# A quantized feed-forward with the gated product on GpSimd and the up projection's copy on ScalarE

## The reference, cut to what matters

```
def fp4_quant_dequant(x):
    xb = x.reshape(shape[:-1] + (shape[-1] // 16, 16))
    scale = jnp.maximum(jnp.max(jnp.abs(xb), axis=-1, keepdims=True) / 6.0, 1e-12)
    idx = jnp.searchsorted(_MID, jnp.abs(xb / scale))
    return (_GRID[idx] * jnp.sign(xb / scale) * scale).reshape(shape)
def fp4_linear(x, w):
    return jnp.einsum('bsk,nk->bsn', fp4_quant_dequant(x), fp4_quant_dequant(w))
gate = fp4_linear(x, w_gate)          # 128 -> 352
y = fp4_linear(x, w_up)               # 128 -> 352
h = jax.nn.silu(gate) * y
return fp4_linear(h, w_down)          # 352 -> 128
x = x + _L1_ffn_ref(_layernorm(x), ...)
```

## Time and profile before

| | us |
|---|---|
| median of 3 runs | 1462.62 (1462.22 to 1463.78) |
| the profiled execution | 1462.41, of which the span 1460.3 |
| TensorE busy in the span | 1284.1 (88%) |
| VectorE | 1015.8 (70%) |
| ScalarE | 931.7 (64%) |
| GpSimd | 510.8 (35%) |
| granted TensorE clock, mean | 0.943 of full speed |

### The profile page before, as it was taken

One profiled execution on the slowest core, in us unless ns is written; L12 is line 12 of the kernel. 1 busy time (PEld: TensorE's weight loads), 2 busy tenths in 40 slices (PEclk: granted clock), 3 DMA queues, 4 the chain that ended last, 5 costly groups with the idle time before them and its releaser, 6 DMA issues.

```text
span 1460.3 us, 17118 instructions
## 1 busy us (share of the span) xinstructions
PE 1284.1 (88%) x6134; PEld 693.6 (47%) x6134; DVE 1015.8 (70%) x1814; ACT 931.7 (64%) x1200; POOL 510.8 (35%) x358
## 2 busy tenths in 40 slices
PE   6999998999899999666878877899989999986666
PEld 3444453445344544331222222477756767763344
DVE  7788858885888578165776778356548676668895
ACT  4999978997899789432565666545545454433321
POOL 1445534553455344417433441023310000006333
PEclk9999999999999999866898999999999999998877
DMA  8100000000000000100000000000010000000000
GB/s 179 48 1 1 0 0 1 0 1 1 0 1 0 0 1 11 63 1 0 1 1 1 1 1 1 1 1 1 1 55 1 1 0 1 1 1 0 1 8 22
DMA packets 27711, 15.01 MB, mean 10 GB/s; under 512 B 16638, under 2 KB 26476, under 8 KB 27500
## 3 DMA queue, kind: packets, MB, share of 16 engines
q1 hardware_dynamic: 27628, 13.92, 3.6%
HBM read 12.86 MB, written 1.05 MB: 10 GB/s over the span
## 4 chain that ended last, share of the span: by engine, by line
PE 36%; issue 24%; POOL 21%; DVE 16%; ACT 2%; POOLq 0%; DMA 0%; SPq 0%; ACTq 0%; DVEq 0%
POOL ARENA L2145 10%; DVE ARENA L874 7%; POOL ARENA L2150 6%; PE PS L749 4%; PE PS L1066 4%; PE PS L732 4%; PE PS L608 3%; POOL ARENA L2157 3%; PE PS L650 3%; PE PS L1074 2%; PE PS L1097 2%; PE PS L617 2%; PE PS L1089 2%; PE PS L1078 2%; PE PS L1751 1%
## 5 line engine op out<-in xcount | busy, mean ns | idle before, releaser
L1751 PE MATMUL PS<-ARENA 128*128 128x512 f32 x512 | 227.3, 597 | 7.5 <-issue 6.7
L874 DVE TENSOR_REDUCE ARENA<-PS 128x1 f32<-128x512 f32 x256 | 160.1, 682 | 69.3 <-PE PS L617 69.1
L2042 DVE TENSOR_SCALAR ARENA<-PS,ARENA 128x512 f32<-128x512 f32 x256 | 188.1, 748 | 27.5 <-PE PS L1751 9.9
L2145 POOL TENSOR_TENSOR ARENA<-ARENA 128x1024 f32<-128x1024 f32 x64 | 151.5, 2367 | 131.6 <-ACT ARENA L1895 126.7
L794 ACT ACTIVATE ARENA<-PS 128x1024 f32<-128x1024 f32 x128 | 129.2, 1026 | 64.3 <-PE PS L636 64.0
L1751 PEld LDWEIGHTS PS<-ARENA 128*128 128x128 f32 x512 | 95.3, 191 | 117.3 <-issue 113.4
L1879 ACT ACTIVATE ARENA<-ARENA 128x2048 f32<-128x2048 f32 x64 | 119.7, 1905 | 47.6 <-DVE ARENA L2042 47.3
L1887 ACT ACTIVATE ARENA<-ARENA,consts_sb 128x2048 f32<-128x2048 f32 x64 | 127.8, 1996 | 0.4
L1760 PE MATMUL PS<-ARENA 128*64 128x512 f32 x512 | 119.9, 611 | 8.1 <-ACT ARENA L1895 8.1
L1895 ACT ACTIVATE ARENA<-ARENA 128x2048 f32<-128x2048 f32 x64 | 118.3, 1897 | 0.0
L617 PE MATMUL PS<-ARENA 32*128 32x512 bf16 x256 | 81.0, 402 | 39.7 <-DVE ARENA L874 27.9
(11 more groups left out here) (257 smaller groups left out, 2611.7 us busy)
## 6 DMA issues: line engine op xcount, KB each, us to landing
ARENA<-in_window_bias_dram SPq DMA_DIRECT2D x1, 1536.0 KB, 6.5
WKVG<-in_L_attn_W_in_dram SPq DMA_DIRECT2D x3, 448.0 KB, 6.7
X<-in_x_dram SPq DMA_DIRECT2D x4, 256.0 KB, 4.4
W<-in_L_ffn_w_dram SPq DMA_DIRECT2D x1, 1024.0 KB
out_dram<-X SPq DMA_DIRECT2D x4, 256.0 KB, 2.2
WQ<-in_L_attn_W_in_dram SPq DMA_DIRECT2D x2, 448.0 KB, 8.3
BV<-in_L_attn_b_in_dram SPq DMA_DIRECT2D x1, 512.0 KB, 6.8
Wout<-in_L_attn_W_out_dram SPq DMA_DIRECT2D x1, 512.0 KB, 4.8
```

Source lines behind the costliest of these rows:

```text
L874: dve.tensor_reduce(NMX[:, w % 2, t, h:h + 1], bank(("cS", n, j)), AX.X, ALU.max, negate=True).then_inc(sem("c_max"), 1)
L1751: done(pe.matmul(o, SK[:, hd, kt * P:(kt + 1) * P], MQ[:, hd, :], start=True, stop=True), ("S", u, c))
L2042: dve.tensor_scalar(D[:, u % 2, hd, kt, :], bank(("S", u, c)), K2[:, u % 2, kt, hd:hd + 1], 1e-30, ALU.add, ALU.max).then_inc(sem("guarded ...
L2145: pool.tensor_tensor(WPAIR, D[:, u % 2, hd, 0:2], D[:, u % 2, hd, 2:4], ALU.add).then_inc(sem("w_paired"), 1)
```

## The change

ScalarE, after the Silu of a step, also copies the up projection out of PSUM, into a new buffer `UF`. It is laid over `W2`, weights of a stage that is over by then. GpSimd forms the product `HF` = `SG` x `UF`, in the new function `product`: those of steps 0 and 1 first, and then in step n that of step n+1 ahead of the subtraction and the multiplication of step n. `HF` gets a second buffer. VectorE no longer forms the product; it waits for `f_h`, which now comes from GpSimd. The banks of `fU` are free after ScalarE's copy (`f_u`) instead of after the product.

```diff
 def gate_and_up_jobs(n):
-    return [(("fG", n), 2, [("f_silu", n + 1)]), (("fU", n), 2, [("f_h", n + 1)])]
+    return [(("fG", n), 2, [("f_silu", n + 1)]), (("fU", n), 2, [("f_u", n + 1)])]
...
-        HF, at = carve(at, [2, FI])
+        HF, at = carve(at, [2, 2, FI])
+        UF = W2[:].rearrange("p e c d -> p (e c d)")[:, 0:4 * FI].rearrange("p (n t f) -> p n t f", n=2, t=2)
...
+            def product(n):
+                pool.wait_ge(sem("f_silu"), n + 1)
+                pool.wait_ge(sem("f_u"), n + 1)
+                if n >= 2:
+                    pool.wait_ge(sem("f_added"), n - 1)
+                pool.tensor_tensor(HF[:, n % 2], SG[:, n % 2], UF[:, n % 2], ALU.mult).then_inc(sem("f_h"), 1)
+
+            product(0)
             for n in range(STEPSF):
 
+                if n + 1 < STEPSF:
+                    product(n + 1)
                 scratch = X_SCRATCH[n % 2]
                 pool.wait_ge(sem("f_added"), n + 1)
...
             act.activation(SG[:, n % 2], bank(("fG", n))[:, :, 0:FI], ACT.Silu).then_inc(sem("f_silu"), 1)
+            full(act, ("fU", n))
+            act.copy(UF[:, n % 2], bank(("fU", n))[:, :, 0:FI]).then_inc(sem("f_u"), 1)
...
         def hidden(dve, link, n, add):
 
-            dve.wait_ge(sem("f_silu"), n + 1)
-            full(dve, ("fU", n))
-            if n:
-                dve.wait_ge(sem("f_added"), n)
-            dve.tensor_tensor(HF, SG[:, n % 2], bank(("fU", n))[:, :, 0:FI], ALU.mult).then_inc(sem("f_h"), 1)
             if n >= 2:
                 add(n - 2)
             dve.wait_ge(sem("f_h"), n + 1)
-            quantize(dve, link, X_SCRATCH[n % 2], P, HF.rearrange("p t n -> p (t n)"), 2 * FI, None, "f_added",
+            quantize(dve, link, X_SCRATCH[n % 2], P, HF[:, n % 2].rearrange("p t n -> p (t n)"), 2 * FI, None, "f_added",
                      max(n - 1, 0))
```

More of the change, by code:

```diff
@@ L560, in decoder_kernel @@
                      "f_rounded", "f_added", "e_exp", "e_rc", "e_p", "e_pt", "e_o", "xb4", "mask_bias",
-                     "f_weights_in", "f_wq", "f_w", "f_yq", "f_x", "f_silu", "f_h", "f_hq", "f_ht", "x_final"):
+                     "f_weights_in", "f_wq", "f_w", "f_yq", "f_x", "f_silu", "f_u", "f_h", "f_hq", "f_ht", "x_final"):
             sem(name)
```

## The result

The changed kernel takes 1481.51 us (median of 4 runs, 1478.99 to 1484.23) against 1463.20 for the kernel before on the same chip: ratio 1.0121, interval 1.0095 to 1.0146, slower by 14 to 21 us. The forecast was 1480.

A forecast was written before the change was run, and what follows sets the result against it. The last stage was taken to go at VectorE's pace; the change closes a serial chain. Start to 1396.6, six turns 64.3, extras 0.8 and 1.5, end 6.15 give 1469.35, 17.6 later: added to the 1462.62 median, 1480; range 1469 to 1488 us.

The forecast's parts named there:

- The closed loop: Last feed-forward stage: one serial chain through four engines, from one step's GpSimd multiplication to the next's, 10.7 us; 63 in 100.
- turn: From the end of one step's GpSimd multiplication to the next's: forecast 10.7 us, against 8.5 before.
- fX: TensorE's transposes ahead of step 5's gate and up matmuls, forecast to add 0.8 us once.
- the input's quantization: VectorE's quantization of the last batch's input, meeting GpSimd's work in one turn: forecast to add 1.5 us once.
- P: The gated product of a step, now on GpSimd: forecast 1.67 us, with 1.39 as the lower end.
- M: GpSimd's multiplication of a step: 1.39 us in the chain; its last end was forecast 17.6 us later.
- the end: From step 6's to step 7's GpSimd multiplication, with no product ahead: VectorE's remaining quantization, subtraction and multiplication, 6.15 us.
- the start: Step 0's GpSimd multiplication, held by step 1's product, forecast to end at 1396.6 instead of 1392.22 us.
- GU: TensorE's eight gate and up matmuls of a step: 3.78 us, ending 4.83 after the earlier GpSimd multiplication.
- S: GpSimd's subtraction of a step, 1.67 us, forecast to wait behind the next step's product, no longer for VectorE's addition.
- The port rival: The port shared by VectorE and GpSimd alone sets the pace in this stage: 7.8 us a step, 1466 us; 5 in 100.
- The hidden product: Rival: GpSimd's product is hidden by running a step ahead, gaining about 5 to 6 us, 1457; 4 in 100.

The follow-up runs named there:

- P behind M: The changed kernel with GpSimd's product for the next step queued behind the current step's multiplication instead of ahead of its subtraction: 1475.65 us, ratio 1.0066.
- P twice: The changed kernel with a second GpSimd product of the same size, into unused columns, ahead of the real one in every step: 1499.56 us, ratio 1.0224.
- copy twice: The changed kernel with ScalarE's copy of the up projection made twice in every step, first into unused columns: 1491.10 us, ratio 1.0165.
- two ahead: The changed kernel with gate and up matmuls, Silu and copy run two steps ahead instead of one: 1471.76 us, ratio 1.0041.
- the open version: The changed kernel with gate and up matmuls two steps ahead and the down projection issued ahead of them: 1468.52 us, ratio 1.0015.

## Why the prediction was right

- *The closed loop.* A turn of 10.7 was forecast; the six took 10.3 to 11.8, 65.7 in all against 66.6 with the fX and the input's quantization. The releasers, the place of P (P behind M), what a longer link costs (P twice, copy twice) and its opening (two ahead: 7.4 a turn) show the cause, not only the size.
- *The terms.* P 1.67, as forecast; the copy 0.75 (0.76); the end 6.0 (6.15); the start 4.1 (4.4). M to the end of GU took 30.4 in the six turns (29.8 with the fX). M started 0.08 behind S and not 0.20: the small instruction of VectorE that was to hold it up ended inside that gap. M(7) moved by 16.3 within the stage, where 17.6 was forecast. The median moved by 18.3; the profiles' other 3.4 arose ahead of the stage, where the one stretch shown, with the same work, was 3.45 longer at a lower granted clock. The forecast had nothing for that and was 1.3 too high in the stage, so the close match of 1480 and 1481.5 is partly luck.
- *The input's quantization*, forecast at 1.5, with P, S and M waiting for VectorE in the turn from M(1) to M(2): they took 2.17, 2.11 and 1.71, 1.3 over their own length.
- *The clock.* I kept the granted clock of before (0.79 in the stretch); it was 0.79 again. That it would be so was a choice and not derived; with P twice it fell to 0.72, and a longer chain would have cost more than its links.
- *VectorE's waits.* I had it wait 3 us or more a step for P. It waited that long, but mostly in front of the addition, for the down projection; for P itself 6.0 us in six steps.
- *The port rival* was over-priced: 7.8 a turn, 7.4 measured, in a stage of 84.8. It named the right engines for the open version: there GpSimd waits 1.95 us a turn for VectorE, whose instructions stretch beside M and P.
- *The hidden product.* When the loop is opened the product is hidden on GpSimd, and its turn is still 0.7 us longer than with the product on VectorE. So the saving of about 5 us did not come in any version run, and by these turns it isn't to be had that way in this stage. With P's place at the start mended as well (3.6 us, from P behind M) I estimate a stage of 81.1 us: 0.7 less than before, and 3.1 more than with the product on VectorE in the same order. That version was not run.

## What to carry to other kernels

When work is moved to an engine "a step ahead", write down what that engine has queued behind it and where its operands come from. If they come from something that the queue itself releases, the step ahead closes a loop, and every engine in it adds its full length. Look at the first step too: there the step ahead cost 4.1 us even in the version with the loop open. Read PSUM as a second chain: a buffer that frees the banks early is what allows matmuls to run ahead, and what TensorE issues behind such matmuls waits with them. And what a moved instruction costs depends on its operands: VectorE's product out of PSUM ran beside GpSimd's subtraction in its usual 0.89 us (at 1434.19, before), while GpSimd's product out of SBUF and VectorE's scaled value and exponent held one another up.

## What the runs showed of the hardware that was not expected

- Excluding instructions on VectorE and GpSimd cost less than their length: an extra 1.36 us product on GpSimd made a clean turn 0.64 longer. And moving the point of exclusion (the product at 2.36 instead of 0.89 us, L1506 at 0.19 instead of 1.08) changed a clean turn by 0.05.
- GpSimd's multiplication of 128x704 took 1.67 us with two different inputs, 1.39 with one of them broadcast over blocks of 16, and 1.36 with the same tensor as both.
- Longer idle times of TensorE went with slower matmuls: 1.67 us more of GpSimd in a turn of 10.9 brought another 1.1 between M and the end of GU, with the granted clock of the stretch at 0.72 instead of 0.79, and 0.64 more of ScalarE brought 0.4.
- The same eight gate and up matmuls took 2.53 to 4.84 us in these profiles, by the level of the clock. In a stage whose engines wait for them that moves single turns by more than 1 us, as much as some of the effects looked for here.
